# GpSimd's gathers: a scrap clear behind each in place of four waits a group

## The chip, the cores and the metric

The kernel runs on one core of a Trainium2 chip. The metric is the device time of one execution in microseconds (us); the time given is the median of three runs.

## What is computed

One layer of graph attention over 6,250 nodes and 100,000 edges, sorted by target node, with 96 features in 8 heads of 12, then a residual and a layer norm:

```python
Q_h, K_h, V_h = x @ Wq + bq, x @ Wk + bk, x @ Wv + bv     # (N, 8, 12) each
E = edge_attr @ We + be                                  # (edges, 8, 12)
score = K_h[src] * Q_h[dst] / sqrt(12) * E
score = exp(clip(score.sum(-1, keepdims=True), -5.0, 5.0))
wV = segment_sum(V_h[src] * score, dst, N)
Z = segment_sum(score, dst, N)
x = layernorm(x + (wV / (Z + 1e-06)).reshape(N, 96))
```

The rows K_h[src] and V_h[src] are fetched for each edge from a table in HBM; that gather is what the change is about.

## The kernel before

**Tables.** TensorE multiplies x, 128 nodes a tile, with the weights of K, V and Q; 25 pairs of tiles. ScalarE copies each pair out of PSUM (line 547), and SyncE stores it to `kv_table` and `q_table` in HBM (lines 401 and 402).

**Groups.** The edges are worked off in 196 groups of 512, a group in 4 tiles of 128 edges (`GROUP_TILES`), 782 tiles in all. For each group:

- SyncE loads the edge features `ea`, the target numbers `rel_bc` and a window of 80 rows of Q (`q_win`); eight groups are on their way at a time.
- GpSimd (POOL in the profile) gathers the K and V rows of the sources into `kv`, one indirect DMA for each tile (line 491), 128 rows of 768 bytes. `kv` is a ring of 16 groups (`KV_RING`).
- ScalarE makes the picking matrix `pick_t` (lines 579, 582), TensorE the features (line 1014, `e_e`) and the picked queries (line 1021, `e_q`), VectorE (DVE) their product (line 742), TensorE turns it (line 1032, `e_turn`), VectorE multiplies it with the gathered keys (line 752), sums by head, clips; ScalarE takes the exponential (lines 593, 594); VectorE weighs the values (line 773, `e_msg`); TensorE sums by node (line 1046, `e_seg`); VectorE adds to `acc_t` (line 788).

VectorE takes the steps of several groups in a fixed order: product of group g, keys of group g-2, weighing of group g-3, adding of group g-5. So every engine waits for the others by semaphores many times a group.

**GpSimd's program.** It has one instruction stream, in order. First 32 early gathers (groups 0 to 7, `EARLY`) of rows of x, from which TensorE makes K and V itself. Then it waits until all tables are stored and takes the groups 8 to 195: groups 16 to 31 wait with `e_msg` until the ring's slot has been used up, and groups from 32 (`PACED_FROM`) are paced instead. Each of a group's four gathers has a wait of its own: for the sums of group g-4, for the features of group g+2, for the picked queries of group g+2, and for the turning of group g.

Of the kernel before, what the change touches and what calls it, by code (L numbers as in the profile page):

```python
# [31 lines left out]
F32 = mybir.dt.float32  # L32
# [7 lines left out]
P = 128  # L40
# [6 lines left out]
GROUP_TILES = 4  # L47
GROUP = GROUP_TILES * P
GROUPS = -(-N_EDGES // GROUP)
# [4 lines left out]
QUADS = GROUPS // QUAD  # L54
WINDOW = 80
EARLY = 8
PACED_FROM = 32

NODE_TILES = -(-N_NODES // P)
TABLE_TILES = NODE_TILES + 1  # L60
# [19 lines left out]
KV_RING, EA_RING, REL_RING, QWIN_RING, PICK_RING, MSG_RING = 16, 8, 8, 8, 4, 4  # L80
# [9 lines left out]
TURNED, WEIGHED, SUMMED, ADDED = 2, 3, 5, 5  # L90
# [4 lines left out]
def tiles_of(group):  # L95
    return min(GROUP_TILES, TILES - group * GROUP_TILES)


def edges_in(tile):
    return min(P, N_EDGES - tile * P)  # L100
# [37 lines left out]
def build(nc, xT, x_rows, src_cols, dst_cols, dst_rows, eaT, weights, biases, ones, out):  # L138
# [9 lines left out]
    assert FINISHED_AFTER[STREAMED_STEPS - 2] + LAG_DIVIDE < GROUPS + 1 == FINISHED_AFTER[STREAMED_STEPS - 1] + LAG_DIVIDE  # L148
    assert STREAMED_STEPS == STEPS - 1 and ADDED == 5 and TURNED == 2 and WEIGHED == 3
    assert SUMS * FINAL_TILES + WINDOW <= 512 and LAG_TRANSPOSE == SUMMED + 2  # L150
    assert KV_RING > 2 * SUMMED and PACED_FROM >= KV_RING
    assert EARLY < KV_RING and tiles_of(EARLY) == GROUP_TILES


# [6 lines left out]
    with ExitStack() as ctx:  # L161
        def sb(name, shape, dt):
            return ctx.enter_context(nc.sbuf_tensor(name, shape, dt))
# [4 lines left out]
        def sem(name):  # L168
            return ctx.enter_context(nc.semaphore(name))
# [66 lines left out]
        rows_f = acc_t[0:PAIRS, 0:2 * GROUP].rearrange("p (j e) -> p j e", j=2)  # L236


        g_src = sb("g_src", [P, GROUP_TILES], U32)
        g_dst = sb("g_dst", [P, GROUP_TILES], U32)  # L240
        g_dst_f = sb("g_dst_f", [P, GROUP_TILES], F32)
# [64 lines left out]
        e_e = sem("e_e")  # L306
        e_q = sem("e_q")
# [3 lines left out]
        e_turn = sem("e_turn")  # L311
# [4 lines left out]
        e_msg = sem("e_msg")  # L316
        e_seg = sem("e_seg")
        e_acc = sem("e_acc")
        g_free = sem("g_free")
        g_idx = sem("g_idx")  # L320
        g_step = sem("g_step")
# [31 lines left out]
        def path_of(eng):  # L353
            eng.wait_ge(r_ready, 1)
            return eng.value_load(path_i[0:1, 0:1], min_val=GENERAL, max_val=STREAMED)
# [6 lines left out]
        def all_tables_stored(eng):  # L362
            for i in range(UNITS_IN_RING):

                eng.wait_ge(d_table[i], 32 * len(range(i, UNITS, UNITS_IN_RING)))

        def by_path(eng, path, windowed, general):

            with eng.If(path == STREAMED):
                windowed(True)  # L370
            with eng.Else():
                with eng.If(path == WINDOWED):
                    windowed(False)
                with eng.Else():
                    general()
# [103 lines left out]
        @block.gpsimd  # L479
        def _(pool):  # L480
            nc.gpsimd.memset(ident[:], 0.0).then_inc(c_id0, 1)
            pool.wait_ge(c_id0, 1)
            nc.gpsimd.affine_select(out=ident[:], in_=ident[:], compare_op=ALU.not_equal, fill=1.0, base=0,
                                    pattern=[[-1, P]], channel_multiplier=1).then_inc(c_ident, 1)
            nc.gpsimd.iota(iota_i[:], pattern=[[1, SPAN]], base=0, channel_multiplier=0).then_inc(c_iota, 1)
            nc.gpsimd.iota(part_i[:], pattern=[[1, 1]], base=0, channel_multiplier=1).then_inc(c_iota, 1)

            def gather(rows, table, group, t, semaphore):
                tile = group * GROUP_TILES + t
                n = edges_in(tile)  # L490
                pool.indirect_dma_start(rows[0:n, :], None, table,  # L491
                                        bass.IndirectOffsetOnAxis(ap=src_idx[0:n, tile:tile + 1], axis=0)
                                        ).then_inc(semaphore, 16)

            pool.wait_ge(l_src_early, 16)
            for group in range(EARLY):
                for t in range(GROUP_TILES):
                    gather(kv[:, group, t, 0:DIM], x_rows, group, t, e_kv[group])
            pool.wait_ge(l_src, 16)
            all_tables_stored(pool)  # L500
            path = path_of(pool)

            def windowed(streamed):
                for group in range(EARLY, GROUPS):
                    slot, ahead = group % KV_RING, min(group + 2, GROUPS - 1)
                    if KV_RING <= group < PACED_FROM:
                        pool.wait_ge(e_msg, group - KV_RING + 1)
                    for t in range(tiles_of(group)):
                        if group >= PACED_FROM:
                            pool.wait_ge(*((e_seg, group - 3), (e_e, ahead + 1), (e_q, ahead + 1), (e_turn, group + 1))[t])  # L510
                        gather(kv[:, slot, t, :], kv_table, group, t, e_kv[slot])

            def general():
                pool.wait_ge(l_dst, 16)
                pool.wait_ge(x_kv, 2 * EARLY)
                with pool.Fori(0, GROUPS) as group:
                    pool.wait_ge(g_free, group + 1)
                    cols = bass.ds(group * GROUP_TILES, GROUP_TILES)
                    nc.gpsimd.tensor_copy(g_src[:], src_idx[:, cols]).then_inc(g_idx, 1)
                    nc.gpsimd.tensor_copy(g_dst[:], dst_idx[:, cols]).then_inc(g_idx, 1)  # L520
                    pool.wait_ge(g_idx, group * 2 + 2)
                    pool.sem_inc(g_step, 1)
                    for t in range(GROUP_TILES):
                        pool.indirect_dma_start(
                            kv[:, 0, t, :], None, kv_table,
                            bass.IndirectOffsetOnAxis(ap=g_src[:, t:t + 1], axis=0)).then_inc(g_gather, 16)
                        pool.indirect_dma_start(
                            g_q[:, t, :], None, q_table,
                            bass.IndirectOffsetOnAxis(ap=g_dst[:, t:t + 1], axis=0)).then_inc(g_gather, 16)

            by_path(pool, path, windowed, general)


# [605 lines left out]
```

## Time and profile before

| | |
|---|---|
| time before, median of 3 runs | 1245.96 us (1243.84 to 1247.04) |
| the profiled execution | 1243.78 us, of which the span from first to last instruction is 1242.0 us |
| TensorE (PE) busy | 818.6 us, 66% |
| VectorE (DVE) busy | 595.4 us, 48% |
| ScalarE (ACT) busy | 458.9 us, 37% |
| GpSimd (POOL) busy | 742.3 us, 60% |
| DMA | 153.24 MB, 123 GB/s over the span |

A row of a timeline gives start, duration, engine, line, operation, tiles written and read, and in brackets how long the engine sat idle before it and what ended that; "remote" is an event that the profile can't put to an instruction of this core, "issue" time in which nothing in the profile was waited for. An indirect DMA is busy on POOL while GpSimd works on it, not until its data has landed.

### The profile page before, as it was taken

Reading aid. Unit: us, or ns where it says so; the run is one execution under the profiler, and the core shown is the slowest. Engines: PE = TensorE matmul, PEld = TensorE weight load, DVE = VectorE, ACT = ScalarE, POOL = GpSimd, SP = SyncE. Lnnn points to the kernel's source line nnn. Section 1 sums busy time; section 2 is a strip of 40 time slices with the busy share of each in tenths; the row PEclk is TensorE's granted clock in tenths of the full one; section 3 lists DMA queues with packets and bytes.
Section 4 is the critical chain, followed back from the end, with each engine's and each line's share of the span. In section 5 each row is a group of like instructions: output and inputs, shape, how many; then the busy total and the mean of one; then the engine's idle time right before and its main releaser. Section 6 shows DMA issues by size and latency. Waiting matters only on the chain.

```text
span 1242.0 us, 13036 instructions
## 1 busy us (share of the span) xinstructions
PE 818.6 (66%) x3375; PEld 451.2 (36%) x3375; DVE 595.4 (48%) x1583; ACT 458.9 (37%) x1094; POOL 742.3 (60%) x790
## 2 busy tenths in 40 slices
PE   4552574797767666667766667766767676676763
PEld 3341242453333333333333433333333333333332
DVE  5010453784444454444544544545454555454545
ACT  1222442563333333333333433433433343334331
POOL 6344456226666656666666666666666666666663
PEclk9685887897877897887888788788887787778785
DMA  9472443455444535444454444454444444444321
GB/s 213 131 206 58 121 127 102 130 139 142 125 130 132 128 106 137 125 119 117 117 135 117 119 131 120 118 135 116 118 123 130 124 124 115 127 125 125 105 73 50
DMA packets 124519, 153.24 MB, mean 123 GB/s; under 512 B 57885, under 2 KB 92191, under 8 KB 124436
## 3 DMA queue, kind: packets, MB, share of 16 engines
q0 software_dynamic: 37008, 75.28, 23.8%
q1 hardware_dynamic: 80608, 73.74, 21.5%
q10 hardware_dynamic: 6822, 3.31, 1.0%
q8 instruction: 31, 0.51, 0.2%
q14 instruction: 50, 0.41, 0.1%
HBM read 142.26 MB, written 9.98 MB: 123 GB/s over the span
## 4 chain that ended last, share of the span: by engine, by line
POOL 26%; PE 26%; issue 19%; another core or an unknown queue 14%; DMA 6%; DVE 4%; ACT 4%; SPq 0%; DVEq 0%; ACTq 0%
POOL kv L491 26%; DMA kv<-kv_table,src_idx 5%; PE ps_eq L1014 5%; PE ps_eq L1021 5%; PE ps_last L1046 3%; PE ps_qe_seg L1046 3%; PE ps_eq_qe L1021 2%; PE ps_eq_qe L1014 2%; PE ps_qe_seg L1032 1%; PE ps_eq_qe L1032 1%; ACT e_t L588 1%; ACT pick_t L582 1%; ACT distance L579 1%; DVE node_stage L734 1%
## 5 line engine op out<-in xcount | busy, mean ns | idle before, releaser
L491 POOL DMA_INDIRECT kv<-kv_table,src_idx x750 | 710.3, 947 | 469.9 <-issue 230.1
L593 ACT ACTIVATE ps_last<-clipped 128x32 f32<-128x32 f32 x196 | 39.4, 201 | 534.1 <-issue 404.5
L1021 PE MATMUL ps_eq<-pick_t,q_win 128*96 128x512 f32 (+1 forms) x262 | 173.3, 750 | 61.5 <-ACT e_t L588 42.7
L1014 PE MATMUL ps_eq<-ea,w_all 128*96 128x512 f32 (+1 forms) x262 | 171.7, 743 | 23.2 <-issue 17.4
L752 DVE TENSOR_TENSOR kq<-kv,ps_qe_seg 128x384 f32<-128x384 f32 x98 | 53.9, 550 | 263.2 <-DMA kv<-kv_table,src_idx 205.3
L752 DVE TENSOR_TENSOR kq<-kv,ps_eq_qe 128x384 f32<-128x384 f32 x98 | 54.1, 552 | 232.4 <-DMA kv<-kv_table,src_idx 191.2
L1046 PE MATMUL ps_qe_seg<-node_stage 128*104 128x80 f32 x784 | 111.7, 298 | 45.9 <-issue 26.5
L579 ACT ACTIVATE distance<-rel_bc,neg_part 80x512 bf16<-80x512 bf16 x196 | 138.4, 706 | 1.6 <-issue 0.5
L1046 PE MATMUL ps_last<-node_stage 128*104 128x80 f32 x780 | 110.2, 296 | 41.6 <-issue 24.3
L582 ACT ACTIVATE pick_t<-distance 80x512 f32<-80x512 bf16 x196 | 123.2, 629 | 6.2
L1046 PEld LDWEIGHTS ps_qe_seg<-node_stage 128*104 128x104 f32 x784 | 100.6, 210 | 55.8 <-issue 43.2
L1046 PEld LDWEIGHTS ps_last<-node_stage 128*104 128x104 f32 x780 | 99.3, 208 | 50.4 <-issue 38.8
L1021 PEld LDWEIGHTS ps_eq<-pick_t,q_win 128*96 128x96 f32 x262 | 49.3, 206 | 176.2 <-issue 175.6
L1021 PE MATMUL ps_eq_qe<-pick_t,q_win 128*96 128x512 f32 x130 | 80.4, 706 | 42.8 <-ACT e_t L588 37.3
L759 DVE TENSOR_REDUCE ps_last<-kq 128x32 f32<-128x384 f32 x196 | 107.5, 549 | 0.1
L773 DVE TENSOR_TENSOR node_stage<-kv,ps_last 128x384 f32<-128x384 f32 x196 | 106.2, 542 | 0.0
L588 ACT COPY e_t<-ps_eq 96x512 f32<-96x512 f32 x131 | 74.6, 569 | 84.2 <-remote 48.1
L742 DVE TENSOR_TENSOR qe_t<-e_t,ps_eq 96x512 f32<-96x512 f32 x131 | 88.3, 674 | 33.7 <-PE ps_eq L1021 22.3
L1032 PE MATMUL ps_qe_seg<-ident,qe_t 96*128 96x96 f32 x390 | 61.0, 288 | 65.5 <-issue 42.0
L1032 PEld LDWEIGHTS ps_qe_seg<-ident,qe_t 96*128 96x128 f32 x390 | 49.7, 167 | 148.1 <-issue 110.4
L1032 PEld LDWEIGHTS ps_eq_qe<-ident,qe_t 96*128 96x128 f32 x392 | 48.7, 161 | 146.8 <-issue 118.5
L1032 PE MATMUL ps_eq_qe<-ident,qe_t 96*128 96x96 f32 x392 | 57.1, 274 | 66.7 <-issue 48.9
(89 smaller groups left out, 720.6 us busy)
## 6 DMA issues: line engine op xcount, KB each, us to landing
ea<-ea_t_in SPq DMA_DIRECT2D x196, 192.0 KB
rel_bc<-rel_rows_dram SPq DMA_DIRECT2D x196, 80.0 KB
kv<-kv_table,src_idx POOLq DMA_INDIRECT x750
q_win<-q_table SPq DMA_DIRECT2D x196, 30.0 KB
kv_table<-node_stage SPq DMA_DIRECT2D x5, 576.0 KB
x_both<-x_t_in SPq DMA_DIRECT2D x5, 480.0 KB, 8.5
x_both<-x_rows_in ACTq DMA_DIRECT2D x10, 240.0 KB
out<-node_stage SPq DMA_DIRECT2D x11, 192.0 KB
```

The costliest lines, as they stand in the source:

```text
L491: pool.indirect_dma_start(rows[0:n, :], None, table, bass.IndirectOffsetOnAxis(ap=src_idx[0:n, tile:tile + 1], axis=0)).then_inc(semaphore ...
L579: nc.scalar.activation(distance[:, b, 0:n], rel_bc[:, slot, 0:n], ACT.Abs, bias=neg_part[0:WINDOW, :]).then_inc(e_dist, 1)
L582: nc.scalar.activation(pick_t[0:WINDOW, group % 3, 0:n], distance[:, b, 0:n], ACT.Relu, bias=1.0, scale=-1.0).then_inc(e_pt, 1)
L588: nc.scalar.copy(e_t[:, group % 2, 0:n], ps_eq[2 * group % 3][0:DIM, 0:n]).then_inc(e_copy, 1)
L742: nc.vector.tensor_tensor(qe_t[:, group % QE_RING, 0:n], e_t[:, group % 2, 0:n], ps_eq[(2 * group + 1) % 3][0:DIM, 0:n], ALU.mult).then_in ...
L752: nc.vector.tensor_tensor(kq[:, group % 2, 0:n, :], kv[:, slot, 0:n, 0:DIM], ps_qe[group % 2][:, 0:n * DIM].rearrange("p (t d) -> p t d", ...
L759: nc.vector.tensor_reduce(score[:, group % 2, 0:n, :], kq[:, group % 2, 0:n, :].rearrange("p t (h d) -> p t h d", h=HEADS), axis=AX_X, op= ...
L773: nc.vector.tensor_tensor(m[:, :, 0:DIM].rearrange("p t (h d) -> p t h d", h=HEADS), kv[:, group % KV_RING, 0:n, DIM:2 * DIM].rearrange("p ...
L1014: nc.tensor.matmul(ps_eq[2 * group % 3][0:DIM, 0:n], w_e, ea[:, slot, 0:n], start=True, stop=True).then_inc(e_e, 1)
L1021: nc.tensor.matmul(ps_eq[(2 * group + 1) % 3][0:DIM, 0:n], q_win[:, slot, :], pick_t[:, group % 3, 0:n], start=True, stop=True).then_inc(e ...
L1032: last = nc.tensor.transpose(ps_qe[group % 2][:, t * DIM:(t + 1) * DIM], qe_t[:, group % QE_RING, t * P:(t + 1) * P], ident[0:DIM, 0:DIM])
L1046: last = nc.tensor.matmul(ps_seg[group % 2][0:SUMS, 0:WINDOW], msg[:, group % MSG_RING, t, :], pick[:, group % PICK_RING, t, :], start=(t ...
```

## The change

Behind every gather GpSimd clears a scrap tile `spacer` of 128 partitions x 128 fp32. Before a clear it waits for the clear before it (`e_space`, which counts them). The four waits of each group from 32 on are gone, and the wait for the ring's slot (`e_msg`), which only groups 16 to 31 had, now stands before the first gather of every group from 16. Nothing else is changed.

```diff
-PACED_FROM = 32
+        spacer = sb("spacer", [P, 128], F32)
+        e_space = sem("e_space")
+            def space(tile):
+                if tile:
+                    pool.wait_ge(e_space, tile)
+                nc.gpsimd.memset(spacer[:], 0.0).then_inc(e_space, 1)
+
             for group in range(EARLY):
                 for t in range(GROUP_TILES):
                     gather(kv[:, group, t, 0:DIM], x_rows, group, t, e_kv[group])
+                    space(group * GROUP_TILES + t)
...
                 for group in range(EARLY, GROUPS):
-                    slot, ahead = group % KV_RING, min(group + 2, GROUPS - 1)
-                    if KV_RING <= group < PACED_FROM:
+                    slot = group % KV_RING
+                    if group >= KV_RING:
                         pool.wait_ge(e_msg, group - KV_RING + 1)
                     for t in range(tiles_of(group)):
-                        if group >= PACED_FROM:
-                            pool.wait_ge(*((e_seg, group - 3), (e_e, ahead + 1), (e_q, ahead + 1), (e_turn, group + 1))[t])
                         gather(kv[:, slot, t, :], kv_table, group, t, e_kv[slot])
+                        space(group * GROUP_TILES + t)
```

On GpSimd, at the early gathers (`iota_i` and `part_i` are constants made before, `l_src_early` tells that the source numbers have been loaded), there stands before:

```order
L485 IOTA iota_i 128x512
L486 IOTA part_i 128x1
L491 DMA kv<-x_rows_in,src_idx 128x96 [waits l_src_early]
L491 DMA kv<-x_rows_in,src_idx 128x96 x31
L355 TENSOR_LOAD path_i [waits d_table2,d_table3,d_table1,r_ready,d_table0,l_src]
```

and in the changed kernel:

```order
L485 IOTA iota_i 128x512
L486 IOTA part_i 128x1
L491 DMA kv<-x_rows_in,src_idx 128x96 [waits l_src_early]
L498 MEMSET spacer 128x128
L491 DMA kv<-x_rows_in,src_idx 128x96
L498 MEMSET spacer 128x128 [waits e_space]
L491 DMA kv<-x_rows_in,src_idx 128x96
```

The 32 gathers that stood next to each other now have a clear between any two, and all but the first clear have a wait.

On GpSimd, group 32, the first that is paced, and the one behind it, before:

```order
L491 DMA kv<-kv_table,src_idx 128x192 [waits e_seg]
L491 DMA kv<-kv_table,src_idx 128x192 [waits e_e]
L491 DMA kv<-kv_table,src_idx 128x192 [waits e_q]
L491 DMA kv<-kv_table,src_idx 128x192 [waits e_turn]
L491 DMA kv<-kv_table,src_idx 128x192 [waits e_seg]
```

and in the changed kernel:

```order
L491 DMA kv<-kv_table,src_idx 128x192 [waits e_msg]
L498 MEMSET spacer 128x128 [waits e_space]
L491 DMA kv<-kv_table,src_idx 128x192
L498 MEMSET spacer 128x128 [waits e_space]
L491 DMA kv<-kv_table,src_idx 128x192
L498 MEMSET spacer 128x128 [waits e_space]
L491 DMA kv<-kv_table,src_idx 128x192
L498 MEMSET spacer 128x128 [waits e_space]
L491 DMA kv<-kv_table,src_idx 128x192 [waits e_msg]
```

A gather's wait for TensorE's work of about the same time has become a wait of GpSimd for itself, and one wait a group for work 16 groups back.

## Rows read from the trace of the kernel before

**Rows 1.** The page: the span, and the chain that ended last by engine.
```profile
span 1242.0 us, 13036 instructions
...
POOL 26%; PE 26%; issue 19%; another core or an unknown queue 14%; DMA 6%; DVE 4%; ACT 4%; SPq 0%; DVEq 0%; ACTq 0%
```

**Rows 2.** Groups by line: count, busy us, mean ns of one, idle before.
```profile
L491 POOL DMA_INDIRECT kv<-kv_table,src_idx x750 | 710.3, 947 | 469.9 <-issue 230.1 <-remote 105.6 <-PE ps_qe_seg L1046 50.1
```

**Rows 3.** Timeline of POOL in the paced stretch, ends of two runs.
```profile
699.89 0.95 POOL L491 DMA_INDIRECT kv<-kv_table,src_idx  x1 [0.30 <-issue]
703.13 0.95 POOL L491 DMA_INDIRECT kv<-kv_table,src_idx  x1 [2.29 <-remote]
...
715.66 0.95 POOL L491 DMA_INDIRECT kv<-kv_table,src_idx  x1 [0.30 <-remote]
719.28 0.95 POOL L491 DMA_INDIRECT kv<-kv_table,src_idx  x1 [2.68 <-PE ps_qe_seg L1032]
```

**Rows 4.** Stretches: length, busy PE, PEld, DVE, ACT, POOL, PEclk, DMA share, GB/s.
```profile
85.00:110.00 25.00, 2.92 (x8) 2.42 (x8) 0.93 (x2) 0.48 (x1) 18.91 (x21) 0.50 0.32 84
300.00:1200.00 900.00, 625.42 (x2507) 329.49 (x2505) 447.60 (x1206) 341.66 (x830) 581.64 (x615) 0.81 0.46 123
```

**Rows 5.** Waits of POOL from 300 to 1200 us: total, times, longest.
```profile
POOL kv L491 <- remote: 104.0, 60, 2.8
```

**Rows 6.** Timeline of POOL: first and last gathers of the runs.
```profile
4.86 1.12 POOL L491 DMA_INDIRECT kv<-x_rows_in,src_idx  x1 [2.77 <-DMA src_idx<-src_cols_in]
...
44.05 0.94 POOL L491 DMA_INDIRECT kv<-x_rows_in,src_idx  x1 [0.30 <-issue]
73.02 0.94 POOL L491 DMA_INDIRECT kv<-kv_table,src_idx  x1 [28.03 <-issue]
...
111.81 0.94 POOL L491 DMA_INDIRECT kv<-kv_table,src_idx  x1 [0.30 <-issue]
131.84 0.94 POOL L491 DMA_INDIRECT kv<-kv_table,src_idx  x1 [19.09 <-DVE node_stage L773]
...
150.61 0.95 POOL L491 DMA_INDIRECT kv<-kv_table,src_idx  x1 [0.30 <-issue]
...
230.86 0.95 POOL L491 DMA_INDIRECT kv<-kv_table,src_idx  x1 [0.31 <-issue]
269.31 0.95 POOL L491 DMA_INDIRECT kv<-kv_table,src_idx  x1 [37.50 <-PE ps_qe_seg L1046]
...
1224.37 0.88 POOL L491 DMA_INDIRECT kv<-kv_table,src_idx  x1 [0.31 <-issue]
```

**Rows 7.** Timeline of DVE while GpSimd rests: the key products of two groups.
```profile
252.21 0.54 DVE L752 TENSOR_TENSOR kq<-kv,ps_qe_seg 128x384 f32<-128x384 f32 x1
...
254.83 0.55 DVE L752 TENSOR_TENSOR kq<-kv,ps_eq_qe 128x384 f32<-128x384 f32 x1
```

**Rows 8.** Timeline of PE, ACT and DVE during the early gathers.
```profile
21.02 1.13 PE L966 MATMUL ps_last<-w_all,x_both 97*128 97x288 f32 x4
...
34.61 0.15 DVE L697 TENSOR_REDUCE room_min<-room 1x1 f32<-1x12 f32 x1 [1.25 <-DVE room L695]
...
42.34 0.64 ACT L547 COPY node_stage<-ps_last 128x576 f32<-128x576 f32 x1 [10.59 <-remote]
...
50.07 0.64 ACT L547 COPY node_stage<-ps_eq 128x576 f32<-128x576 f32 x1 [7.09 <-remote]
```

**Rows 9.** Timeline of ACT after two runs of gathers.
```profile
118.19 0.86 ACT L554 COPY kv<-ps_eq_qe 128x384 f32<-128x384 f32 x2 [0.25 <-remote]
...
154.62 0.58 ACT L588 COPY e_t<-ps_eq_qe 96x512 f32<-96x512 f32 x1 [16.32 <-remote]
```

**Rows 10.** Timeline of POOL at the start of the program.
```profile
0.75 0.20 POOL L481 MEMSET ident<- 128x128 f32 x1 [0.29 <-POOLq L1131]
1.20 0.28 POOL L483 TENSOR_SCALAR_AFFINE_SELECT ident<-ident 128x128 f32<-128x128 f32 x1 [0.24 <-POOL ident L481]
1.45 0.55 POOL L485 IOTA iota_i<- 128x512 int32 x1
```

More of the change, by code:

```diff
@@ L150, in build @@
     assert SUMS * FINAL_TILES + WINDOW <= 512 and LAG_TRANSPOSE == SUMMED + 2
-    assert KV_RING > 2 * SUMMED and PACED_FROM >= KV_RING
     assert EARLY < KV_RING and tiles_of(EARLY) == GROUP_TILES
```

## The prediction

> **What bounds the kernel now.** I read the page's chain first, then the groups by line, the waits of GpSimd, and its instructions in order of time. The chain that ends last is spread over many short steps, with GpSimd's gathers (POOL) and the matmuls as its two largest shares, 26% each [rows 1]; a chain so broken up is a loop in which the engines wait for one another. The gathers are 782: 32 early ones of x, and 750 of kv_table at 947 ns each [rows 2]. Back to back they start every 1.25 us, the 0.95 of the gather and 0.30 before it [rows 3]. Between 300 and 1200 us, 900 us hold 615 gathers, 581.6 us busy [rows 4]; 104.0 us of the rest go to 60 waits for a "remote" event, one that the profile can't name [rows 5]. From gather 97 of kv_table at 269.31 to the last, at 1224.37, there are 653 intervals in 955.1 us, **1.463 us a gather** [rows 6], or 5.85 us a group of four. The compute can do better: where no gather runs (231.8 to 269.3), the key product of VectorE comes every 2.62 us [rows 7], a group each.
>
> So the paced stretch is bound by the gathers at 1.463, not at 1.25. Why not 1.25 is the question, and the trace answers it where the gathers run unpaced. In the first run, 32 of them back to back from 4.86 to 44.99, TensorE has finished the table product of pair 7 at 22.1 us, but ScalarE copies it out at 42.34; the next copy, which waits in the program only for the product that follows that one on TensorE, comes at 50.07, 5.1 us after the gathers have stopped [rows 8]. VectorE even waits 1.25 us for its own previous instruction, one gather's period [rows 8]. The next 32 end at 112.76 and ScalarE is released last at 118.19, 5.4 us later; 16 end at 151.56 and ScalarE moves at 154.62, 3.1 us later, after 16.3 us at rest [rows 6, 9]. In the paced stretch a run of 9 (from 689.89) ends at 700.84 and the next gather is released at 703.13, 2.3 us later; a run of 11 ends at 716.61 and the next comes at 719.28, 2.7 us later [rows 3]. **The wake-ups of all engines come late by an amount that grows with the run**: from 2.3 us after 9 to some 5.25 after 32 is 2.95 us in 23 gathers, 0.13 us a gather. I read this as something that serves a gather in 1.25 + 0.13 = 1.38 us (an estimate; call it 1.39) and passes the engines' signals through the same line. The data engines aren't it: in the stalled stretch 85 to 110 they are 32% busy [rows 4].
>
> **The change part by part.** (1) The waits of groups 32 and later on e_seg, e_e, e_q and e_turn go, and the ring's e_msg takes their place for all groups from 16: a gather then waits for work 16 groups back. By itself this removes no time from the gathers' own 1.25, and would bring back the ring-bound run of the start: 64 gathers from 131.84 to 230.86, 63 intervals in 99.0 us, **1.57 each** [rows 6], worse than paced, since the late wake-ups hold the compute and the compute then holds the ring.
>
> (2) Each gather gets a clear of 128 x 128 fp32 behind it. The wait in front of that clear is for the clear before it, a whole gather earlier, so as a rule it is met; behind it on GpSimd stands the next gather only, and for that DVE waits. The price is the clear's time in the period. The nearest row is the clear of ident, the same size, 0.20 us [rows 10]. Upper bound: a wait of GpSimd for its own last instruction costs 0.24 (the select behind that clear) [rows 10], so 0.95 + 0.30 + 0.20 + 0.24 = 1.69. Lower bound: the 0.30 ahead of a gather hides the clear whole, and the period stays 1.25 [rows 3]. I take 0.95 + 0.30 + 0.20 = **1.45**, since two instructions on GpSimd that don't wait for each other follow without a gap (the iota starts at 1.45, before the select's end at 1.48) [rows 10] and nothing says that the gather's 0.30 shrinks.
>
> The Trainium skill, Perfetto Trace Analysis, GPSIMD Engine Instruction, says that spans on this engine are unreliable and that the spacing of starts is to be used. By that the clear would add less than 0.20 and the period would lie nearer 1.35; the overlap of select and iota agrees with it, and what follows is where that would end.
>
> At a period under 1.39 the line of signals grows again, until the clear's own completion comes late, the wait in front of the next clear is no longer met, and GpSimd is held to 1.39. So low prices of the clear all end at 1.39: the wait paces the gathers by itself.
>
> (3) At 1.45 the growth of 0.13 a gather is covered by the 0.20 of the clear (margin 0.06), so I expect prompt wake-ups. Groups then come every 5.8 us where 2.62 suffices, the compute follows the gathers, and the ring never holds: its waits cost nothing as long as that is so; if the cover is gone the price is rival A's.
>
> (4) The start. In before the kv gathers begin at 73.02, since the tables are late; two of the ScalarE copies, at 42.34 and 50.07, wait 10.6 and 7.1 us for an event that can't be named [rows 8]. With prompt wake-ups the tables are bounded by the early gathers, now 4.86 + 32 x 1.45 = 51.3. Between 51.3 and 73.0 I take **55**, near the lower end, because once the run is over, the 17 copies left of 25 and all their stores take only the 23 us from 50.07 to 73.02 [rows 6, 8]. Group 0's compute then starts long before group 16 needs its slot, so the 19 us stop before 131.84 and the 38 us stop before 269.31 [rows 6] go too.
>
> (5) The tail: last gather to the end of the span is 1242.0 - 1224.4 = 17.6 us [rows 1, 6], the landing, the last group and the last nodes; it stays.
>
> **Sum**, against the profiled execution (span 1242.0, 1243.78 outside, 2.2 under the median of 1245.96): 55 + 749 x 1.45 + 17.6 + 1.8 = 55 + 1086.1 + 19.4 = 1160.5; by the median's offset **1162 us**, 6.7% faster. Of the 83 us, 73.0 + 96 x 1.45 = 212 against 269 for the first 96 gathers is 57, the earlier start is 18, and 1.463 against 1.45 over 653 gathers is 8. Bounds: at 1.39 and a start at 52, 52 + 1041 + 19.4 = 1112; at 1.69, the early gathers end at 59, 59 + 1266 + 19.4 = 1344. The break-even with before is a period of (1243.8 - 19.4 - 55) / 749 = **1.56**.
>
> **The rivals.** A, *the gap does not clear the line* (slower): what makes wake-ups late is not served by an idle GpSimd of 0.2 us but needs the pauses of 2 us and more that pacing gave. Then the kernel runs as it did from 131.84 on, stalled and ring-bound: 73 + 749 x 1.57 + 19.4 = 1268. It decides where lateness still grows by over 0.1 us a gather. For it: in the paced stretch, pauses of that length are there. Against: lateness grew by only 0.13 a gather.
> The Trainium skill, DMA: Bandwidth & Descriptors, Issuing engines are not separate DMA queues, says that the transfers of all queues run on the same 16 engines and interleave. Were the lateness that sharing, the same bytes would be moved and A's 1268 would come out; the 32% busy of rows 4 speak against it.
>
> B, *the clear costs its whole chain* (slower): GpSimd pays dispatch, 0.20, a self-wait and the gather's 0.30 in series, 1.69 a gather, 1344; it decides from 1.56. For it: the self-wait of 0.24 is a row. Against: the awaited clear is a gather old.
>
> C, *nothing is won at the start*: the line is full anyway, 1.463 is its rate under all signals, and the tables stay late: 73 + the old first stretch, about 1240, no change.
>
> D, *the clear hides in the 0.30*: GpSimd is held to 1.39 by its own wait, 52 to 55 + 1041 + 19.4 = 1112 to 1115, with wake-ups late by up to 1.3 us, which 5.6 us a group can bear.
>
> **How the numbers follow.** My forecast, a period of 1.40 to 1.52 with a start at 52 to 65: 0.57. D: 0.13. C: 0.07, most of it no change. A: 0.12. B, down to periods of 1.57: 0.11. The time is the forecast's, 1162. The range takes in D and A and cuts B's upper part: 1110 to 1290. About 0.3% is what a measurement tells from no change: faster 0.72, within 0.04, slower 0.24 (A, B and a little of C).
>
> **What would show it.** Right: clears of about 0.2 us between gathers whose starts lie 1.45 apart, all the way; the first kv gather at about 55; no ScalarE wait of over 5 us in the first 60 us; GpSimd's waits for "remote" and e_msg near zero; its share in the chain over half; the key product still waiting for the gather's landing. Wrong: a start spacing over 1.56 (B); gathers in bursts with stops of 4 to 7 us that end on DVE's weighted values, the e_msg signal, and ScalarE at rest for 16 us (A); the first kv gather still near 73 (C); a spacing of 1.39 with the spacer as releaser of GpSimd's waits (D). My prediction is wrong from the ground if lateness isn't a matter of the gathers' spacing but of their number in flight.

## The result, and the profile after

The changed kernel takes 1306.5 us (median of 4 runs, 1300.5 to 1309.2) against 1244.9 us of the kernel before (1243.1 to 1247.0) in the same sitting: a ratio of 1.0485, interval 1.0461 to 1.0510, so **4.9% slower**. The prediction was 1162 us, 1110 to 1290, faster. The profiled execution took 1300.45 us.

The page: the span and the chain that ended last, against [rows 1].

```profile
span 1298.6 us, 13818 instructions
...
another core or an unknown queue 36%; PE 23%; issue 17%; DVE 12%; ACT 10%; DMA 1%; DVEq 0%; SPq 0%; ACTq 0%
```

GpSimd had 26% of the chain and now has none; events that the profile can't name rose from 14% to 36%. The gathers are no longer the bound. The timeline of GpSimd at the first gathers of kv_table, at one stop, and at the end (start, duration, engine, line; in brackets the idle time before and what ended it):

```profile
49.08 0.22 POOL L498 MEMSET spacer<- 128x128 f32 x1
66.03 0.95 POOL L491 DMA_INDIRECT kv<-kv_table,src_idx  x1 [16.73 <-issue]
66.98 0.22 POOL L498 MEMSET spacer<- 128x128 f32 x1
67.37 0.95 POOL L491 DMA_INDIRECT kv<-kv_table,src_idx  x1 [0.17 <-issue]
...
697.01 0.95 POOL L491 DMA_INDIRECT kv<-kv_table,src_idx  x1 [0.17 <-issue]
697.97 0.22 POOL L498 MEMSET spacer<- 128x128 f32 x1
703.19 0.95 POOL L491 DMA_INDIRECT kv<-kv_table,src_idx  x1 [5.00 <-DVE node_stage L778]
...
1241.01 0.88 POOL L491 DMA_INDIRECT kv<-kv_table,src_idx  x1 [0.17 <-issue]
```

Undisturbed, gathers start 1.34 us apart (66.03, 67.37): the clear stands directly behind the gather, and the idle time ahead of the next gather has shrunk from the 0.30 of [rows 3] to 0.17. But from 66.03 to 1241.01 there are 749 intervals in 1175.0 us, 1.569 each, since the runs end in stops like the one before 703.19, on e_msg, the ring. GpSimd's waits, whole span and from 300 to 1250 us (total, times, longest):

```profile
POOL kv L491 <- DVE node_stage L778: 170.8, 42, 10.2
```

```profile
POOL kv L491 <- DVE node_stage L778: 137.4, 34, 6.6
```

No wait for the spacer is in that list: the clear's own signal is never late. The time adds up from three pieces: before, 73.0 to the first gather of kv_table, 749 x 1.537, and 17.6 of tail; now 66.0, 749 x 1.569, and 57.6 (1298.6 - 1241.0). So the start gained 7.0 us, the gathers lost 23.6, and **the tail lost 40.0**: at the last gather VectorE has 15 groups left to weigh (line 778), nearly the whole ring of 16, and weighs the last at 1286.0; in the kernel before 3 were left.

Why it is behind shows on the other engines, ahead of that stop (PE, ACT and DVE, timeline from 677 to 699):

```profile
677.42 0.49 PE L1037 MATMUL ps_eq_qe<-ident,qe_t 96*128 96x96 f32 x4
677.75 0.88 PE L1051 MATMUL ps_last<-node_stage 128*104 128x80 f32 x8
678.47 1.04 PE L1019 MATMUL ps_eq_qe<-ea,w_all 128*96 128x512 f32 x2
682.56 1.07 PE L1026 MATMUL ps_eq<-pick_t,q_win 128*96 128x512 f32 x2 [3.05 <-issue]
...
684.77 0.68 DVE L747 TENSOR_TENSOR qe_t<-e_t,ps_eq 96x512 f32<-96x512 f32 x1 [2.64 <-PE ps_eq L1026]
...
687.65 0.56 DVE L757 TENSOR_TENSOR kq<-kv,ps_eq_qe 128x384 f32<-128x384 f32 x1 [2.20 <-remote]
...
696.17 0.24 DVE L793 TENSOR_TENSOR acc_t<-acc_t,ps_last 104x80 f32 x1 [6.54 <-remote]
...
698.93 0.58 ACT L593 COPY e_t<-ps_eq_qe 96x512 f32<-96x512 f32 x1 [14.99 <-remote]
```

TensorE finished the features in ps_eq_qe at 679.5; the copy that reads them and waits for nothing else (e_e) starts at 698.93, 19.4 us later and 1.0 us after the run's last gather has ended. In between, the turned queries that TensorE finished in ps_eq_qe at 677.91 reached VectorE at 687.65, 9.7 us late, and the segment sums of 678.63 in ps_last reached it at 696.17, 17.5 us late; VectorE was idle for the last 2.2 and 6.5 us of these. But the picked queries in ps_eq, finished at 683.63, released VectorE at 684.77, after 1.1 us. VectorE's own chain (kq, sum, clip) runs without a gap from 687.65 to 689.62. So the late ones are TensorE's signals, by very different amounts, and a later one overtakes earlier ones.

The kernel before has the same in its first run of gathers. The copy at 50.07 of [rows 8] reads this product, which ends at 23.12:

```profile
21.99 1.13 PE L966 MATMUL ps_eq<-w_all,x_both 97*128 97x288 f32 x4
```

So that signal took 27.0 us. There, with gathers 1.25 us apart, VectorE's signals to itself were late too (the wait of 1.25 us in [rows 8]); in the changed kernel the same instruction follows without a wait:

```profile
32.17 0.15 DVE L702 TENSOR_REDUCE room_min<-room 1x1 f32<-1x12 f32 x1
```

ScalarE's waits for the copy of the features, before and after:

```profile
ACT e_t L588 <- remote: 68.3, 24, 16.3
```

```profile
ACT e_t L593 <- remote: 590.6, 91, 16.4
```

### The profile page after: what moved, and what is told of

Same layout as the page of the kernel before. It is cut to its first block, busy times and chain, and to the rows that moved or that the text cites. A ratio compares the mean times of both kernels' runs of the same rounds, so it can differ in the third digit from the quotient of the medians.

```text
span 1298.6 us, 13818 instructions
## 1 busy us (share of the span) xinstructions
PE 773.1 (60%) x3375; PEld 453.2 (35%) x3375; DVE 598.9 (46%) x1583; ACT 455.8 (35%) x1094; POOL 919.5 (71%) x1572
## 3 DMA queue, kind: packets, MB, share of 16 engines
q0 software_dynamic: 37008, 75.28, 22.0%
q1 hardware_dynamic: 80608, 73.74, 20.4%
## 4 chain that ended last, share of the span: by engine, by line
another core or an unknown queue 36%; PE 23%; issue 17%; DVE 12%; ACT 10%; DMA 1%; DVEq 0%; SPq 0%; ACTq 0%
PE ps_eq L1026 5%; PE ps_eq L1019 3%; ACT distance L584 3%; ACT pick_t L587 3%; PE ps_eq_qe L1026 2%; DVE ps_last L764 2%; PE ps_qe_seg L1051 2%; DVE node_stage L739 2%; PE ps_last L1051 2%; PE ps_eq_qe L1019 2%; ACT e_t L593 2%; PE ps_qe_seg L1037 2%; DVE qe_t L747 2%; DVE kq L757 2%
## 5 line engine op out<-in xcount | busy, mean ns | idle before, releaser
L1026 PE MATMUL ps_eq_qe<-pick_t,q_win 128*96 128x512 f32 x130 | 88.9, 773 | 162.5 <-issue 119.9
L498 POOL MEMSET spacer<- 128x128 f32 x782 | 172.8, 221 | 0.4
L1019 PE MATMUL ps_eq<-ea,w_all 128*96 128x512 f32 (+1 forms) x262 | 152.8, 667 | 23.7 <-issue 21.2
L593 ACT COPY e_t<-ps_eq_qe 96x512 f32<-96x512 f32 x65 | 37.4, 575 | 225.0 <-remote 182.4
L1051 PE MATMUL ps_last<-node_stage 128*104 128x80 f32 x780 | 105.5, 289 | 2.9 <-DVE acc_t L793 1.5
L1051 PEld LDWEIGHTS ps_qe_seg<-node_stage 128*104 128x104 f32 x784 | 104.5, 216 | 0.8 <-issue 0.8
L1026 PEld LDWEIGHTS ps_eq_qe<-pick_t,q_win 128*96 128x96 f32 x130 | 21.8, 195 | 210.3 <-issue 210.3
L739 DVE TENSOR_TENSOR node_stage<-ps_last,rel_f 128x320 f32<-128x320 f32 x196 | 94.3, 481 | 0.5 <-ACT ps_last L598 0.5
L1019 PE MATMUL ps_eq_qe<-ea,w_all 128*96 128x512 f32 x130 | 81.6, 715 | 2.7 <-issue 1.7
```

Of the source, the lines that this page charges most:

```text
L498: nc.gpsimd.memset(spacer[:], 0.0).then_inc(e_space, 1)
L593: nc.scalar.copy(e_t[:, group % 2, 0:n], ps_eq[2 * group % 3][0:DIM, 0:n]).then_inc(e_copy, 1)
L739: nc.vector.tensor_tensor(pick[:, group % PICK_RING, 0:n, :], window_iota.unsqueeze(1).to_broadcast([P, n, WINDOW]), rel.unsqueeze(2).to_b ...
L1019: nc.tensor.matmul(ps_eq[2 * group % 3][0:DIM, 0:n], w_e, ea[:, slot, 0:n], start=True, stop=True).then_inc(e_e, 1)
L1026: nc.tensor.matmul(ps_eq[(2 * group + 1) % 3][0:DIM, 0:n], q_win[:, slot, :], pick_t[:, group % 3, 0:n], start=True, stop=True).then_inc(e ...
L1051: last = nc.tensor.matmul(ps_seg[group % 2][0:SUMS, 0:WINDOW], msg[:, group % MSG_RING, t, :], pick[:, group % PICK_RING, t, :], start=(t ...
```

## The experiments

The runs were made in six sittings after the first; all kernels of one are timed beside the kernel before. That kernel took 1227.2 us in sitting A (e1 to e4), 1228.0 in B (e5 to e8), **1006.9 in C (e9 to e11) and 1006.7 in D (e12 to e14)**, 1238.6 in E (e15 to e17) and 1228.7 in F (e18), within 0.5% in each. C and D show no late signal in any kernel, the others do. C and E were on a chip of the same number (2), some 14 minutes apart, and are of different kinds, so the chip by itself does not decide it; what does, no run here tells.

### The spacing: no clear, 256, 384 and 320 columns

e1 takes the clears out and leaves the ring; the others change the width.

```diff
-                        space(group * GROUP_TILES + t)
```
```diff
-        spacer = sb("spacer", [P, 128], F32)
+        spacer = sb("spacer", [P, 256], F32)
```

> The changed kernel without its clears: gathers back to back every 1.25 us, only the ring of 16 groups holds them. Theory S (spacing: each gather needs a hidden service of about 1.40 us, of which lateness is the part not covered by the spacing): ring-bound throughout, at least the 1.57 us a gather of the first ring-bound stretch of before, start at 73, so 73 + 749 x 1.57 + 57 = 1306 us or more, up to 1340; the early ScalarE copies late again by 5 us. Theory N (lateness comes from gathers queued without a pause, whatever their spacing between 1.25 and 1.5): the clears changed nothing in the stalled loop, and the time equals the changed kernel's within 1%, 1295 to 1320. Gain of the clears in the early stage by either: 73 against 66, 7 us.

> The changed kernel with clears twice as wide, 256 columns: period 1.336 + 128 x 0.93 ns x 2 halves = about 1.45 us. Theory S: lateness doesn't grow any more at 1.45, the stalls vanish, and GpSimd is the bound: start near 57, 57 + 749 x 1.45 + 20 = 1163, between 1155 and 1185 us; waits of ScalarE for unnamed events under 5 us. Theory N: still ring-bound at about 1.57, 1290 to 1320 us, with stops of 4 to 7 us on the ring.

> Clears of 384 columns: period about 1.57 us, all of it on GpSimd. Theory S: no stalls, compute prompt, start near 60, 60 + 749 x 1.57 + 20 = 1256, between 1240 and 1275 us, tail under 22 us. Theory N: stalls on top of the period, above 1300 us, tail of 40 us or more.

> Clears of 320 columns, a spacing of about 1.50 us. If the need of a gather lies at 1.45 or just under, signals are prompt: 56 + 749 x 1.50 + 19 = 1198 us, tail under 25 us. If it lies above 1.50: signals late by 1 us and more, tail of 40 us and more, 1215 to 1240 us.

| kernel | us | ratio to before (interval) | undisturbed spacing | tail |
|---|---|---|---|---|
| e1, no clear | 1320.1 | 1.0756 (1.0709 to 1.0803) | 1.25 | 57 |
| e2, 256 columns | 1201.7 | 0.9789 (0.9764 to 0.9813) | 1.447 | 58 |
| e8, 320 columns | 1197.7 | 0.9752 (0.9732 to 0.9771) | 1.497 | 17 |
| e3, 384 columns | 1238.4 | 1.0091 (1.0070 to 1.0113) | 1.550 | 17 |

ScalarE's waits for the features (total, times, longest) in e1, e2 and e8:

```profile
ACT e_t L591 <- remote: 524.3, 71, 15.1
```

```profile
ACT e_t L593 <- remote: 419.8, 105, 5.9
```

```profile
ACT e_t L593 <- remote: 10.3, 10, 1.6
```

In e3 ScalarE has no such wait at all. The chain of e8, and of e2:

```profile
POOL 87%; issue 11%; DVE 1%; DMA 1%; PE 0%; ACT 0%; POOLq 0%; DVEq 0%
```

```profile
PE 45%; issue 19%; another core or an unknown queue 18%; ACT 10%; POOL 4%; DVE 3%; DMA 1%; ACTq 0%; DVEq 0%; POOLq 0%
```

From 1.50 on the gathers are the bound, the tail is short and the sum of my prediction holds with the row's own spacing: e8's first gather at 54.3, 749 x 1.500, tail 17, 1194.6 of span. At 1.447 there is a state that I had not thought of: GpSimd hardly ever stops (3 waits on the ring, 3.7 us), yet nearly every signal of TensorE comes late, by a steady few us, all the way; the compute just holds the gathers' pace, a ring behind, and pays for it with the tail. Theory S is right in kind (spacing cures), and the need in the loop is above 1.45, not the 1.39 of the prediction or the 1.40 of these expectations. It is not one number for all stages: in the same sitting A, 1.336 was enough for the early gathers (with the clears of 128 columns in e4 the first gather of kv_table comes at 50.1, without them in e1 at 69.7).

Two other causes drop out by these runs, GpSimd's load and TensorE's clock. GpSimd is busier where the signals are prompt (1045.6 us in e8, 88% of the span) than where they are late (919.5 us, 71%, in the changed kernel). The granted clock of TensorE was 0.82 in the profiled executions of both e2, where signals are late, and e8, where they are not.

### The mean, or the single gap

e7 puts the same mean spacing into one clear a group.

```diff
-        spacer = sb("spacer", [P, 128], F32)
+        spacer = sb("spacer", [P, 960], F32)
...
-                        space(group * GROUP_TILES + t)
+                    space(group)
```

> One clear of 960 columns behind each group of four gathers instead of one of 256 behind each gather: the mean spacing is the same 1.45 us, but in a group the gathers are 1.25 us apart and then comes one gap of about 0.8 us more. Theory S (only the mean spacing counts): as with 256 columns, signals 1 to 3 us late, compute a ring of groups behind, tail of about 58 us, 1195 to 1210 us. Theory P (a signal needs one gap that is long enough): prompt once a group, compute keeps up, tail near 18 us, 1155 to 1170 us. Theory R (each gather needs its gap): stalls on the ring again, above 1250 us.

1193.5 us, 0.9723 (0.9699 to 0.9746); the profiled execution, at 1184.5 the fastest of five, has a mean of 1.448 and a tail of 46. Its gathers, three at 1.25 and then the gap:

```profile
603.81 0.95 POOL L491 DMA_INDIRECT kv<-kv_table,src_idx  x1 [0.30 <-issue]
605.06 0.95 POOL L491 DMA_INDIRECT kv<-kv_table,src_idx  x1 [0.30 <-issue]
606.32 0.94 POOL L491 DMA_INDIRECT kv<-kv_table,src_idx  x1 [0.31 <-issue]
607.25 0.92 POOL L498 MEMSET spacer<- 128x960 f32 x1
608.34 0.95 POOL L491 DMA_INDIRECT kv<-kv_table,src_idx  x1 [0.17 <-issue]
```

ScalarE still waits 378.1 us in 104 times for events without a name. The time lies just under the range of S and far from those of P and R: the mean counts, the single gap hardly.

### What a gather takes: rows, bytes, or one gather

```diff
-                n = edges_in(tile)
+                n = edges_in(tile) if group < KV_RING else min(edges_in(tile), P // 2)
```
```diff
-                        gather(kv[:, slot, t, :], kv_table, group, t, e_kv[slot])
+                        gather(kv[:, slot, t, 0:DIM], x_rows, group, t, e_kv[slot])
```

In e6 the weighing, too, reads the half that is fetched (that part of the edit isn't shown).

> The changed kernel, clears of 128 columns kept, but gathers of groups from 16 on fetch 64 rows instead of 128 (the other 64 rows of kv keep what an earlier group left, so part of the result isn't computed). Theory D (what a gather takes from the hidden line is set by its rows, one descriptor each): the need falls to about half, 0.7 us, under the spacing; signals of TensorE prompt, no stop on the ring, GpSimd the bound at its spacing of 1.34 us or less: 60 + 749 x 1.34 + 20 = 1084 us or less. Theory G (a gather takes a fixed time of the line, whatever it fetches): stalls as in the changed kernel, 1.50 us a gather or more, 1250 to 1310 us.

> The changed kernel, clears of 128 columns kept, but every gather of the loop fetches 128 rows of 384 bytes (from the rows of x) instead of 768 bytes; the values aren't weighed with their own numbers, so the result isn't the reference's. Theory T (bytes on the transfer engines make the signals late): stalls go, 60 + 749 x 1.336 + 20 = 1080 us. Theory D (rows) and G (a fixed time): nothing changes, 1.55 us a gather or more, 1280 to 1310 us.

Half the rows: 1307.5 us, 1.60 us a gather. Half the bytes: 1283.1 us, 1.567 a gather, 174.9 us of stops on the ring. Each was run once, and is 1.065 and 1.045 of the kernel before in B; the changed kernel itself was run in the first sitting (1.0485) and in C only. The software queue's bytes fell from 75.28 to 40.04 and 38.45 MB, and the stalls stayed, so neither the rows nor the bytes of a gather make the signals late (the half gathers of e5 are 0.04 us shorter and so start 1.29 us apart, a little closer than before). The third candidate was SyncE's traffic:

```diff
-                        if group >= EA_RING:
-                            sp.wait_ge(e_dist, group - REL_RING + 1)
-                            load_rows(group)
-                            sp.wait_ge(e_q, group - EA_RING + 1)
-                            load_features(group)
-                        load_window(group, base)
+                        if group < QWIN_RING:
+                            load_window(group, base)
```

ScalarE's and TensorE's waits for the dropped loads are set to the first load of each slot (not shown).

> The changed kernel, but SyncE loads features, window rows and queries for the first 8 groups only, and the later groups compute with those (so nearly all of the result isn't computed); 3 of the transfers of a group go, the gathers and all signals between engines stay. Theory G (a gather alone takes 1.45 us of the hidden line): still starved at 1.336, 1.5 us a gather or more, 1230 to 1300 us. Theory L (the line is shared by SyncE's transfers, 3 a group, which take the rest of the 1.45): signals prompt at 1.336, 50 + 749 x 1.336 + 20 = 1071 us.

> The same kernel without SyncE's loads after the 8th group, since the chip of the first try showed no late signal in any kernel. On a chip where the kernel before takes over 1200 us: theory G (a gather alone needs 1.45 to 1.5 us): 1.5 us a gather or more, 1240 to 1300 us; theory L (SyncE's transfers share the line): prompt, 50 + 749 x 1.336 + 20 = 1071 us. On a chip where the kernel before takes 1007 us: 1071 us by both, and nothing is told apart.

> Once more without SyncE's loads after the 8th group. Only a chip with over 1200 us for the kernel before tells apart: theory G 1240 to 1300 us, theory L 1071 us. On a chip with 1007 us: 1069 to 1071 us by both.

In sittings C and D it told nothing (1070.5 and 1068.9 us, as the whole kernel there). In E, 1283.5 us in one run, 1.036 of before, 1.545 a gather, and the stops are nearly what they were (the page's queues with packets, MB and share, then the wait on the ring):

```profile
q0 software_dynamic: 37008, 75.28, 22.4%
q1 hardware_dynamic: 23456, 15.56, 4.7%
```

```profile
POOL kv L487 <- DVE node_stage L774: 154.3, 35, 9.9
```

With the other queue's 73.74 MB down to 15.56, TensorE's signals are still late: theory L falls. G's range is met, but that a gather alone takes a fixed 1.45 to 1.5 us isn't shown: 1.336 was enough early in A, and 1.25 in C and D. The Trainium skill, DMA: Bandwidth & Descriptors, Issuing engines are not separate DMA queues, says that DMAs started by different engines run on the same 16 DMA engines and interleave. If the delay were that sharing alone, half of the gathers' bytes (e6) or a fifth of the other queue's (e16) should have made it much shorter; the stops stayed.

### The clears alone, and the ring alone

e4 is the kernel before, paced waits and all, with clears of 128 columns behind every gather.

```diff
                         gather(kv[:, slot, t, :], kv_table, group, t, e_kv[slot])
+                        space(group * GROUP_TILES + t)
```

> The kernel before, with its paced waits, and the clear of 128 columns behind every gather: the clears alone. Theory S: a paced loop whose period of 5.85 us a group is set by runs of gathers and late wake-ups, with 0.086 us less lateness a gather and 0.086 us more on GpSimd: same or some faster, 1215 to 1250 us. Theory N: the clear adds its 0.086 us to each of 650 gathers, up to 56 us, 1250 to 1300 us. In both the early stage gains up to 7 us.

> The changed kernel without its clears, only the ring of 16 groups. On a chip where the kernel before takes 1007 us (no late signals): gathers at 1.25 without a stop, 51 + 749 x 1.25 + 20 = 1007 us, the same as before within 0.5%, so that the 64 us of the change there are the clears alone. On a chip with over 1200 us: about 1.58 us a gather, 1300 to 1325 us, as in the first run of it.

e4: 1216.2 us, 0.9896 (0.9865 to 0.9927). e15: 1333.3 us, 1.0775 (1.0725 to 1.0824), e1's result again. So, where signals are late, of the two parts of the change the clears are a small gain and **giving up the paced waits costs 7.6 to 7.8%**, of which clears of 128 columns give back too little. e4 also shows where the paced kernel loses: its paced stretch runs at 1.450 a gather, but two stops at the start, 23.0 us before group 16 and 39.4 before group 32, come from the unpaced groups.

### Where no signal is late

> The changed kernel itself, beside the others on this chip, where the kernel before takes 1227 us instead of 1245. If what the first pair of runs showed is the change and not the chip: 1.03 to 1.06 of before, 1.57 us a gather, a tail of 57 us. The start may differ: the first gather of kv_table at 66 on the first chip, at 50 in the three kernels with the same early clears here; at 50 the time would be 50 + 749 x 1.57 + 58 = 1284 us.

> The kernel before itself, for its trace on this chip. On a chip with 1007 us: signals prompt everywhere, gathers at 1.25 without a stop, 50 + 749 x 1.25 + 20 = 1006 us, the paced waits met before they are reached. On a chip with over 1200 us: the paced loop again at 1.45 to 1.47 us a gather, first gather of kv_table at 66 to 73.

e9, the changed kernel in sitting C: 1070.8 us against 1006.9, 1.0634 (1.0616 to 1.0652). Its first and last gathers of kv_table (span 1069.0), and those of e14, the kernel before in sitting D (1007.4 us, span 1005.5):

```profile
50.05 0.95 POOL L491 DMA_INDIRECT kv<-kv_table,src_idx  x1 [1.38 <-issue]
...
1051.54 0.88 POOL L491 DMA_INDIRECT kv<-kv_table,src_idx  x1 [0.17 <-issue]
```

```profile
50.56 0.94 POOL L491 DMA_INDIRECT kv<-kv_table,src_idx  x1 [4.05 <-issue]
...
987.84 0.88 POOL L491 DMA_INDIRECT kv<-kv_table,src_idx  x1 [0.30 <-issue]
```

That is 1.337 and 1.251 a gather, without one stop of the ring or of the pacing over 0.4 us; the clears cost their 0.086 x 749 = 64 us and there is nothing to cure. The change is slower in both kinds of sitting, for two different reasons.

### A better version

e11, e13 and e17 try 288 columns (128 behind the early gathers):

```diff
-                nc.gpsimd.memset(spacer[:], 0.0).then_inc(e_space, 1)
+                nc.gpsimd.memset(spacer[:, 0:128 if tile < EARLY * GROUP_TILES else 288], 0.0).then_inc(e_space, 1)
```

> The version that the runs point to: clears of 128 columns behind the 32 early gathers (where 1.336 us is enough on this chip) and of 288 behind the others, a spacing of 1.472. If the need lies under 1.47: signals prompt, 51 + 749 x 1.472 + 19 = 1173 us, 0.955 of before. If it lies between 1.47 and 1.50: signals 1 to 2 us late as with 256 columns, tail of 45 to 58 us, 1195 to 1212 us.

> Clears of 128 columns early and 288 later once more. On a chip where the kernel before takes over 1200 us: 1173 us if the need lies under 1.47, 1195 to 1212 if over it. On a chip where it takes 1007: 1171 us again, GpSimd's own spacing and nothing else.

> Clears of 128 columns early and 288 later. On a chip with over 1200 us for the kernel before: 1173 us if the need lies under 1.47, 1195 to 1212 if over it. On a chip with 1007 us: 1170 us.

1170.6 and 1170.2 us in C and D (16% over before there), 1227.1 us in E, 0.9891 (0.9857 to 0.9926). In E its 1.470 is still too close, with ScalarE waiting as in e2 and a tail of 59 us, and the 1.336 of its early gathers is late there too (first gather of kv_table at 66.3, where e4 in A had 50.1): the spacing that is enough is not the same in all sittings. Of the two widths run in both kinds of sitting, 128 and 288, neither is good in both.

e18 keeps the pacing, which adapts, from group 16 instead of 32, and has clears of 384 columns only where nothing paces yet, behind groups 0 to 15.

```diff
-PACED_FROM = 32
+PACED_FROM = 16
...
+        spacer = sb("spacer", [P, 384], F32)
...
                     gather(kv[:, group, t, 0:DIM], x_rows, group, t, e_kv[group])
+                    space(group * GROUP_TILES + t)
...
                         gather(kv[:, slot, t, :], kv_table, group, t, e_kv[slot])
+                        if group < PACED_FROM:
+                            space(group * GROUP_TILES + t)
```

> The kernel before with its paced waits from group 16 on (instead of 32) and clears of 384 columns behind the gathers of groups 0 to 15 only: prompt signals while nothing paces, no clear afterwards. Where the kernel before takes 1227 to 1245 us: the first gather of kv_table at 57, group 16 at 57 + 32 x 1.55 = 107 without a stop, then 717 x 1.463 + 19: 1175 us, 0.94 to 0.96 of before. If the paced loop can't start from a short lead and stops at group 16: 1200 to 1230. Where the kernel before takes 1007: 107 + 717 x 1.25 + 20 = 1023 us, 1.6% slower than before.

**1167.8 us, 0.9515 (0.9491 to 0.9540).** Its gathers:

```profile
58.66 0.95 POOL L493 DMA_INDIRECT kv<-kv_table,src_idx  x1 [0.32 <-issue]
...
112.63 0.95 POOL L493 DMA_INDIRECT kv<-kv_table,src_idx  x1 [4.43 <-PE ps_qe_seg L1056]
113.88 0.95 POOL L493 DMA_INDIRECT kv<-kv_table,src_idx  x1 [0.30 <-issue]
...
1147.69 0.88 POOL L493 DMA_INDIRECT kv<-kv_table,src_idx  x1 [0.30 <-issue]
```

58.7 to the first, one stop of 4.4 at group 16 in place of the 19 and 38 of [rows 6], then 717 intervals in 1035.1 us, 1.444 each, and 17.4 of tail. So the start can be mended without touching the paced rate. By its own sum it would cost some 16 us over before where signals are prompt; that wasn't run.

## Why the prediction was wrong, step by step

- **What bounds before**: right. The paced stretch is held at its 1.463 by late signals; where they aren't late (e14) the same kernel runs at 1.251.
- **(1) The pacing goes**: right in size. The ring alone gives 1.589 and 1.594 a gather (e1, e15) where I put 1.57. What I left out for that case is the tail.
- **(2) The price of the clear**: wrong term. P was 0.95 + 0.30 + 0.20 = 1.45; it is 0.95 + 0.22 + 0.17 = 1.336. Behind a clear of any width the gap ahead of the gather is 0.17, so 0.13 of the 0.30 hides under it and a clear costs its time less 0.13. I had written that nothing says that the 0.30 shrinks. The Trainium skill, Perfetto Trace Analysis, GPSIMD Engine Instruction, says to time such instructions by the spacing of their starts and not by the reported spans. The 1.35 that I put beside it was my own estimate; the starts came 1.336 apart, and I didn't follow it.
- **Held to 1.39 by its own wait**: wrong. The spacer's signal is never late (no such wait in any list), so nothing on GpSimd pushes back, and rival D falls with it.
- **(3) The cover**: the step that decided. I read wake-ups that come 2.3 to 5.4 us late as a backlog of 0.13 us a gather, served in order, and so a need of 1.38 to 1.39. The need is over 1.45 (e2, e7), over 1.47 in sitting E, and at most 1.50 in B (e8). Even P = 1.45 as predicted would not have been prompt: e2 and e7 have just that mean, and took 1202 and 1193 us. Nor is it a backlog in order: signals overtake one another, and at 1.447 they are late without growing for a thousand us. The lateness after a run's end, from which I took the slope, doesn't measure what a signal waits within the run: the one of 27.0 us above stands in the slope with 5.1. Why signals are late, and what sets the need, stays open.
- **(4) The start**: predicted 55, measured 66.0, of before's 73.0; three of ScalarE's early copies still wait 5 us each for events without a name, where [rows 8] had 10.6 and 7.1. At 384 columns it is 57.0 and at 320 54.3, so the mechanism was right and the cover too thin in that sitting; in A and B the same early clears gave 50.1 to 50.6 (e4, e5, e6).
- **(5) The tail stays**: wrong by 40 us, the largest single piece of the loss against before. I counted it as landing, last group and last nodes, which holds only when the compute isn't behind.
- Against the sum: start +11, gathers 749 x 0.119 = +89, tail +40, together the 140 us that are missing (the sum with its offset of 2.2 is 1162.7, put down as 1162).
- **Rival A** happened, by the signs I gave for it: stops of 4 to 7 us on e_msg, one of 10 early on, and ScalarE at rest for 16. Its 1268 had 1.57 right and lacked the 40 us of tail. Its mechanism is only half right: the 0.2 us of this clear is too little, but no pause of 2 us is needed, since e8's clear of 320 columns, with a spacing of 1.50, is enough. Its chance of 0.12 was too low: the case that 0.2 us is enough rested on one slope from five lateness readings, and the whole forecast held only as long as the need lay under 1.45, 0.06 from my estimate of it.
- **C** put the start at 73, where it came at 66, and was wrong on the rate, which wasn't the line's limit of 1.463 but the stops' 1.569; **B** failed (1.336, not 1.69).
- **Wrong from the ground**, if not the spacing but the number of gathers in flight counted: the spacing does count (e2, e3, e8), but no run changes it and the number in flight apart from each other.

## What to carry to other kernels

A wait that paces by what the consumers have done adapts to whatever delays them; a fixed filler has to be sized for the worst sitting and is paid in the best. Before a pacing wait is taken out, ask what its pauses were for, and whether the replacement gives as much mean room, not just some. And when a producer may run a ring ahead of consumers that can't keep up, the tail of the kernel grows by what the ring holds.

## What the hardware showed that was not expected

- A run of gathers delays TensorE's signals to ScalarE and VectorE, by 19.4 us in the changed kernel's stop above and by 27.0 in the first run of the kernel before. In the changed kernel's loop, VectorE's signals to itself, GpSimd's, and those from ScalarE to TensorE (the copy that starts at 698.93 releases the product at 699.65) come at once; with gathers 1.25 us apart, VectorE's own were late too. Halving the rows or the bytes, or cutting the other queue's traffic to a fifth, does not end the delay; a wider mean spacing of the gathers does, late at 1.45 (A, B) and 1.47 (E), prompt at 1.50 (B). What the signals wait for stays open.
- In two sittings of seven there was no such delay at all, and the same kernel took 1007 us instead of 1227 to 1245. One of the two was on a chip that, by its number, has the delay in another sitting, so it isn't the chip alone; what it is stays open. A figure for the worth of pacing holds for one kind of sitting only.
- The 0.30 us between two gathers is 0.17 behind a clear of 128 to 960 columns. The time of a clear: 0.22, 0.33, 0.44 and 0.92 us for 128, 256, 384 and 960 columns.
